# Two transformer layers on one core: GpSimd splits two early weight chunks and the router's weights first, and the other three early chunks after the layer norm

## The chip, the cores and the metric

The kernel runs on 1 core of a Trainium2 chip. The metric is the device time of one execution in microseconds (us), the median of several. The core has a matrix engine (TensorE, PE in the profile, with PEld for its weight loads), VectorE (DVE), ScalarE (ACT), GpSimd (POOL) and SyncE (SP), which here only issues DMA transfers. Each engine works through its own list of instructions in order, and waits on semaphores for the others.

## The reference, cut to what matters

Two layers, each an attention and a feed-forward part, each part added to its input and normalised (layer norm) behind it. Batch 2, sequence 1024, width 256, all in float32. The change lies at the end of the second layer's attention and the start of its feed-forward part, a mixture of experts:

```python
x = _layernorm(x + _L0_attn_ref(x, ...))
x = _layernorm(x + _L0_ffn_ref(x, W1, W2, W3))
x = _layernorm(x + _L1_attn_ref(x, Wq, bq, Wk, bk, Wv, bv, Wo, bo))
x = _layernorm(x + _L1_ffn_ref(x, w12, w3, router_w, expert_bias, sw1, sw2, sw3))

# _L1_ffn_ref
g = x @ sw1.T                                  # shared expert, 1024 wide
u = x @ sw2.T
shared_out = jax.nn.silu(g) * u @ sw3.T
scores = jax.nn.sigmoid(x @ router_w.T)        # router, 8 experts
_, top_idx = jax.lax.top_k(scores + expert_bias, 2)
...                                            # each token goes through its 2 experts, 128 wide
return shared_out + routed_out
```

## The kernel before

The two sequences of the batch are computed one after the other (`for b in range(B)`, B = 2); "batch 0" and "batch 1" below are these two passes. A pass holds 1024 rows of 256 in SBUF (`X`, 8 tiles of 128 rows) and goes through first attention, first feed-forward, second attention, second feed-forward. The order of the work on each engine is written out by hand, one block of code per engine.

**Products in three passes.** A float32 operand is split in a high part (rounded to the matrix engine's fp32r type) and a low part (the rest), and a product is the sum of high x high, high x low and low x high (`pass3`, lines 409 to 411). The high part is a cast, the low part a subtraction. So every weight has to be split before it is used: `Fw_h`, `Fw_l` are the parts of a feed-forward chunk, `E_h`, `E_l` of an expert, `Rw_h`, `Rw_l` of the router's weights, `XT_h`, `XT_l` of the transposed rows, `H_h`, `H_l` of the hidden values.

**The feed-forward chunks.** Both feed-forward parts go through chunks of 128 hidden columns: chunks 0 to 7 are the first part, 8 to 15 the second part's shared expert. A chunk (gate, up and down weights, 128x768) is loaded into `Fw_raw[c % 2]`, two buffers in turn, and split into one of five `Fw_h`, `Fw_l` slots. `load_chunk(b, c, ...)` on SP (line 693) waits until the chunk two before it has been split (`fw_lo`), since that one lay in the same buffer, and then issues two transfers (lines 695, 696). `EARLY` (line 87) names chunks 8 to 12: both their parts are made by GpSimd in `ffn_split` (line 2293, the cast on 2297, the subtraction in the helper `low` on 2255) at the end of the second attention. Chunks 13 to 15 are split later by ScalarE and VectorE.

**SP's list around the change** (lines 765 to 776): the loads for the second attention, the five `EARLY` chunks, then a wait for the residual sum (`z_done`), the router's constants `moe` and `tri_raw` (770, 771), the experts' weights `E_raw` in four transfers of two experts each (774), and chunks 13 to 15:

```python
for c in EARLY:
    load_chunk(b, c, d["fb"][c - CH_F0])
sp.wait_ge(z_done, LN_B * b + 3 * NT)
...
    sp.dma_start(E_raw[:, e], d["fe"][e].rearrange("e p n -> p e n")).then_inc(er_in[i], 16)
```

**The layer norm behind the second attention.** VectorE's `attn1_out` calls `add_norm`: for each of 8 tiles it adds the projected attention to `X` (`residual`, line 1662) and takes statistics (1667); after tile 5 it normalises tiles 0 to 3 (`layernorm(b, 2, 0)`, line 1683, four instructions, each raising `ln_done`), and after tile 7 it makes `XT_l` of the first 512 rows (`x_parts`, 1658) and normalises tiles 4 to 7. PE transposes normalised tiles in between (`transpose_x`, 816). While it has nothing else it issues products that are thrown away (`keep_clock`, 802).

**The shared expert.** Steps s = 16 to 31 (`S_SHARED` = 16) go over chunks 8 to 15: 16 to 19 are chunks 8 to 11 on the first 512 rows, 20 to 23 the same chunks on the other rows. PE's `ffn` (line 986): `gate_up(16)`, `gate_up(17)`, transposes of the other 512 rows, `gate_up(18)`, `router` (which waits in `wait_xt` for `XT_l` of the other rows, and for `rw_lo`), `down(16)`, `gate_up(19)`, and so on. ScalarE's `ffn` for each step: `silu` (1470); at step 17 also `x_parts` (1330, `XT_h` of the other 512 rows); `hidden_high` (1475); and for steps 16 to 19 `split_experts` (1505), which waits for transfer i of `E_raw` (`er_in`) and casts two experts. VectorE makes the products of gate and up (`Hf`, 1870), `XT_l` (1658) and `H_l` (1874). GpSimd makes `E_l`, and later issues the scatter of the tokens to their experts.

Of the kernel before, what the change touches and what calls it, by code (L numbers as in the profile page):

```python
# [35 lines left out]
NT = T // P  # L36
# [50 lines left out]
EARLY = range(CH_F0, CH_F0 + FW_RING)  # L87
# [8 lines left out]
def program(nc, d, ctx):  # L96
    def sem(name):
        return ctx.enter_context(nc.semaphore(name))

    def sb(name, shape, dt=F32, scope=ctx):  # L100
        return scope.enter_context(nc.sbuf_tensor(name, shape, dt))
# [111 lines left out]
    Rw_raw = sb("Rw_raw", [P, KC, P], F32, s)  # L213
    Rw_h = sb("Rw_h", [P, KC, P], F32R, s)
    Rw_l = sb("Rw_l", [P, KC, P], F32R, s)
# [53 lines left out]
    rw_in = sem("rw_in")  # L269
# [11 lines left out]
    ln_done = sem("ln_done")  # L281
# [54 lines left out]
    rw_hi = sem("rw_hi")  # L336
    rw_lo = sem("rw_lo")
# [272 lines left out]
    LN_B = 4 * NT  # L610
# [1642 lines left out]
    def _(pool):  # L2253
        def low(dst, full, high):
            return nc.gpsimd.tensor_tensor(dst, full, high.bitcast(F32), ALU.subtract)
# [13 lines left out]
        def attn0_group(b, g, last):  # L2269
            it = b * GROUPS0 + g  # L2270
            for n in range(STEPS0):
                w = (q_tile(n, last) + 1) * P
                e1, e2 = E1[n % 2][:, 0:w], E2[n % 2][:, 0:w]
                pool.wait_ge(mix_ready, STEPS0 * it + n + 1)
                pool.nop(nofuse=True)
                nc.gpsimd.tensor_scalar(e2, e2, mixc[:, n % 4:n % 4 + 1], 1.0, ALU.mult,  # L2276
                                        ALU.mult).then_inc(mix_scaled, 1)
                pool.wait_ge(mix_scaled, STEPS0 * it + n + 1)
                nc.gpsimd.tensor_tensor(e1, e1, e2, ALU.add).then_inc(p_ready, 1)  # L2279
                for t in v_tiles(n):  # L2280
                    pool.wait_ge(v_hi, NT * it + t + 1)
                    low(V_l[:, t, :].unsqueeze(1), O[:, t, bass.ds(g % 2 * 2 + 1, 1), :],
                        V_h[:, t, :].unsqueeze(1)).then_inc(v_lo, 1)
                if n in SPLIT_STEPS:
                    split_wa(it + 1, SPLIT_STEPS.index(n))
                if last and n == STEPS0 - 2:
                    scale_wo(it)
            if not last:
                scale_wo(it)
            pool.wait_ge(wo_hi, it + 1)  # L2290
            low(Wo_l[:], Wo_raw[:], Wo_h[:]).then_inc(wo_lo, 1)

        def ffn_split(b, c):
            if c in EARLY:
                pool.wait_ge(fw_in[c % 2], CHUNKS * 16 * b + (c + 2 - c % 2) * 16)
                pool.nop(nofuse=True)
                nc.gpsimd.tensor_copy(Fw_h[c % FW_RING][:], Fw_raw[c % 2][:]).then_inc(fw_early, 1)
                pool.wait_ge(fw_early, FW_RING * b + c - EARLY[0] + 1)
            else:
                pool.wait_ge(fw_hi, (CHUNKS - FW_RING) * b + (c if c < CH_F0 else c - FW_RING) + 1)  # L2300
            low(Fw_l[c % FW_RING][:], Fw_raw[c % 2][:], Fw_h[c % FW_RING][:]).then_inc(fw_lo, 1)
# [62 lines left out]
        for b in range(B):  # L2364
            attn0_group(b, 0, False)
            with pool.Fori(1, GROUPS0 - 1) as g:
                attn0_group(b, g, False)
            if b == 0:
                pool.wait_ge(const_in, CONSTS * 16)
            pool.wait_ge(y_added, 3 * NT * b + (GROUPS0 - 2) * NT)  # L2370
            add_bias(0)
            attn0_group(b, GROUPS0 - 1, True)
            attn0_out(b)
            ffn0(b)
            nc.gpsimd.memset(causal[:, 0:HALF - P], 0.0).then_inc(filled, 1)
            nc.gpsimd.tensor_copy(causal[:, HALF - P:], mask_r[:].bitcast(F32)).then_inc(filled, 1)
            pool.wait_ge(wv_hi, b + 1)
            low(Wv_l[:], Wv_raw[:], Wv_h[:]).then_inc(wv_lo, 1)
            split_wb(b)
            for n in range(NT):  # L2380
                pool.wait_ge(v1_done, NT * b + n + 1)
                values = Vs[:, n, :, 0:D1]
                nc.gpsimd.tensor_tensor(values, values, rows_bc[:, 2, :].rearrange("p (h e) -> p h e", h=HEADS1),
                                        ALU.add).then_inc(vb_done, 1)
            for p in range(PAIRS1):
                for j in CUT:
                    cut_future(PAIRS1 * b + p, p, j)
                    if j == CUT[0]:
                        if p == 0:
                            pool.wait_ge(xt_ps, LN_B // 2 * b + 12)  # L2390
                        add_tile_bias(p)
            for c in EARLY:
                ffn_split(b, c)
            pool.wait_ge(rw_in, 16 * b + 16)
            pool.wait_ge(rw_hi, b + 1)
            low(Rw_l[:], Rw_raw[:], Rw_h[:]).then_inc(rw_lo, 1)
            pool.wait_ge(moe_in, 32 * b + 32)
            pool.nop(nofuse=True)
            nc.gpsimd.tensor_copy(tri[:], tri_raw[:, 0:2 * P].rearrange("p (c n) -> p c n", c=2)).then_inc(tri_done, 1)
            nc.gpsimd.tensor_copy(X[:, :, HID], tri_raw[:, 2 * P:]).then_inc(tri_done, 1)  # L2400
            for e in range(EXPERTS):
                pool.wait_ge(er_hi, EXPERTS * b + e + 1)
                low(E_l[:, e], E_raw[:, e], E_h[:, e]).then_inc(er_lo, 1)
            pool.wait_ge(tri_done, 2 * b + 2)
            pool.wait_ge(xs_init, 16 * b + 16)
            pool.wait_ge(rt_dve, R_B * b + R_PLACE)
            pool.nop(nofuse=True)
            for t in range(NT):
                for c in range(TOP):
                    nc.gpsimd.indirect_dma_start(d["xs"], bass.IndirectOffsetOnAxis(place_i[:, c, t:t + 1], 0), X[:, t, :],  # L2410
                                                 None).then_inc(sc_out, 16)
            for k in range(TILES):
                if k in [ends[0] for ends in XG_LOADS]:
                    load = [ends[0] for ends in XG_LOADS].index(k)
                    pool.wait_ge(dest_done, 3 * len(XG_LOADS) * b + 3 * load + 3)
                    pool.nop(nofuse=True)
                pool.wait_ge(ry_copy, TILES * b + k + 1)
                pool.nop(nofuse=True)
                nc.gpsimd.indirect_dma_start(d["ys"], bass.IndirectOffsetOnAxis(dest_i[:, k:k + 1], 0), xg[:, k, 0:HID],
                                             None).then_inc(yr_out, 16)  # L2420
# [84 lines left out]
```

## Time and profile before

| | before |
|---|---|
| median of 3 runs | 1646.4 us |
| lowest and highest | 1642.59, 1650.22 us |
| the profiled execution: its own time | 1648.83 us |
| its span, first to last instruction | 1647.1 us |
| mean granted TensorE clock, share of full | 0.989 |
| busy: PE, DVE, ACT, POOL | 1542.6, 1101.2, 930.0, 695.7 us |

The profile is of one execution. Its page gives each engine's busy time and groups instructions by line; the timeline gives single instructions (or merged ones, with "x4") with their start, their time and, in brackets, how long the engine sat idle before and what released it; a view of windows gives busy time and the granted clock (PEclk, 1.00 is 2.4 GHz, 0.50 is 1.2 GHz) of stretches. The end of the second attention lies at 677 to 697 us for batch 0 and at 1489 to 1509 us for batch 1.

### The profile page before, as it was taken

To read this page: it belongs to the slowest core of one execution; us is meant where nothing else is said; L and a number is where in the kernel's file an instruction comes from. 1 tells how busy PE (TensorE), PEld (TensorE's weight loads), DVE (VectorE), ACT (ScalarE), POOL (GpSimd) and SP (SyncE) were. 2 spreads that over 40 slices of the span, in tenths; PEclk is the share of its full clock that TensorE was granted. 3 is DMA by queue.
4 is the path that set the end of the run, shared out by engine and by line. 5 is a ranking of instruction groups with operands and counts; after the bars stand their busy time and mean duration, and the time that the engine had idled before them with its cause. 6 is when DMAs were issued, how large, how long until landed. Compare 5 with 4: busy or idle time off the path is not lost.

```text
span 1647.1 us, 30890 instructions
## 1 busy us (share of the span) xinstructions
PE 1542.6 (94%) x10614; PEld 1331.6 (81%) x10614; DVE 1101.2 (67%) x2705; ACT 930.0 (56%) x2054; POOL 695.7 (42%) x756
## 2 busy tenths in 40 slices
PE   8999999999999999899898999999999999998985
PEld 7888889888888677588788898898988876667784
DVE  6767667677745888474577676676766377865555
ACT  5666565665544577552566655556554347774352
POOL 1635444654560222451535445444554512226531
PEclk9999999999999999999999999999999999999998
DMA  3110000020110422223210200000202123313133
GB/s 132 46 52 17 27 1 16 25 91 1 49 60 13 80 50 45 64 103 126 101 68 6 73 18 26 16 25 0 91 1 68 40 41 64 52 32 130 62 123 103
DMA packets 48195, 88.02 MB, mean 53 GB/s; under 512 B 9600, under 2 KB 30480, under 8 KB 46928
## 3 DMA queue, kind: packets, MB, share of 16 engines
q1 hardware_dynamic: 43552, 75.28, 15.9%
q0 software_dynamic: 3744, 10.26, 1.7%
q8 instruction: 76, 1.25, 0.3%
q10 hardware_dynamic: 768, 0.79, 0.2%
q14 instruction: 55, 0.45, 0.1%
HBM read 60.18 MB, written 19.76 MB: 49 GB/s over the span
## 4 chain that ended last, share of the span: by engine, by line
PE 64%; DVE 15%; ACT 10%; issue 7%; POOL 3%; ACTq 0%; DMA 0%; DVEq 0%; POOLq 0%; SPq 0%
PE ps L409 16%; PE ps L411 15%; PE ps L410 15%; PE ps L1214 4%; PE ps L1196 4%; PE ps L1161 3%; ACT E L1411 3%; DVE nmax L1810 3%; PE ps L924 2%; ACT PT L1572 2%; POOL E L2279 2%; DVE On L1728 2%; ACT PT_h L1393 1%; DVE PT_l L1785 1%; POOL E L2276 1%
## 5 line engine op out<-in xcount | busy, mean ns | idle before, releaser
L1411 ACT ACTIVATE E<-ps,nmax 128x128 f32<-128x128 f32 (+7 forms) x256 | 189.1, 741 | 208.5 <-DVE nmax L1810 208.1
L2276 POOL TENSOR_SCALAR E<-E,mixc 128x128 f32<-128x128 f32 (+7 forms) x128 | 97.1, 759 | 399.7 <-DVE mixc L1778 399.7
L1810 DVE TENSOR_REDUCE nmax<-ps 128x1 f32<-128x128 f32 (+7 forms) x256 | 183.3, 749 | 12.7 <-PE ps L901 12.6
L2279 POOL TENSOR_TENSOR E<-E 128x128 f32<-128x128 f32 (+7 forms) x128 | 182.4, 1425 | 10.7
L1572 ACT ACTIVATE PT<-ps 128x512 f32<-128x512 f32 x288 | 153.9, 602 | 57.3 <-PE ps L1196 56.5
L409 PE MATMUL ps<-V_h,PT_h 128*128 128x256 f32 x576 | 167.3, 290 | 1.7 <-DVE O L1790 1.7
L410 PE MATMUL ps<-V_l,PT_h 128*128 128x256 f32 x576 | 163.1, 283 | 0.0
L411 PE MATMUL ps<-V_h,PT_l 128*128 128x256 f32 x576 | 163.0, 283 | 0.0
L409 PE MATMUL ps<-K_h,Q_h 128*128 128x512 f32 (+3 forms) x384 | 147.4, 384 | 8.9 <-ACT E L1411 5.6
L2337 POOL TENSOR_SCALAR_AFFINE_SELECT PT<-PT 128x256 f32<-128x256 f32 (+1 forms) x160 | 57.0, 361 | 202.3 <-ACT PT L1572 201.0
L1785 DVE TENSOR_TENSOR PT_l<-ps,PT_h 128x128 fp32r<-128x128 f32 (+7 forms) x128 | 96.7, 756 | 60.7 <-ACT PT_h L1393 60.1
L411 PE MATMUL ps<-K_h,Q_l 128*128 128x512 f32 (+3 forms) x384 | 133.2, 347 | 0.0
L410 PE MATMUL ps<-K_l,Q_h 128*128 128x512 f32 (+3 forms) x384 | 132.7, 346 | 0.0
L2030 DVE CUSTOM_DVE_ANT_0 masked<-ps,causal 128x128 bf16<-128x128 f32 (+3 forms) x256 | 110.4, 487 | 33.3 <-PE ps L1161 33.1
L1161 PE MATMUL ps<-KS,QS 128*128 128x512 f32 (+3 forms) x384 | 114.2, 374 | 2.3 <-DVE nmax_part L2030 0.6
L409 PEld LDWEIGHTS ps<-V_h,PT_h 128*128 128x128 f32 x576 | 109.8, 191 | 3.5 <-issue 2.1
L1196 PE MATMUL ps<-QS,KS 128*128 128x512 f32 (+3 forms) x384 | 108.7, 363 | 3.0 <-ACT PT L1572 2.9
L410 PEld LDWEIGHTS ps<-V_l,PT_h 128*128 128x128 f32 x576 | 110.0, 191 | 0.5
L411 PEld LDWEIGHTS ps<-V_h,PT_l 128*128 128x128 f32 x576 | 109.8, 191 | 0.0
L409 PE MATMUL ps<-XT_h,Fw_h 128*128 128x512 f32 x256 | 103.7, 405 | 4.9 <-DVE XT_l L1658 2.2
L1870 DVE TENSOR_TENSOR Hf<-ps,silu_g 128x512 f32<-128x512 f32 x64 | 44.2, 691 | 91.5 <-PE ps L411 77.2
L411 PE MATMUL ps<-XT_h,Fw_l 128*128 128x512 f32 x256 | 102.2, 399 | 1.0 <-issue 1.0
(265 smaller groups left out, 4659.7 us busy)
## 6 DMA issues: line engine op xcount, KB each, us to landing
Wa_raw<-in_wa SPq DMA_DIRECT2D x8, 1024.0 KB, 6.0
Fw_raw<-in_fa SPq DMA_DIRECT2D x32, 256.0 KB, 2.6
E_raw<-in_fe SPq DMA_DIRECT2D x8, 768.0 KB, 7.3
xs<-in_xs SPq DMA_DIRECT2D x2, 2967.0 KB, 13.0
Wo_raw<-in_wo SPq DMA_DIRECT2D x8, 512.0 KB, 3.5
yg<-ys SPq DMA_DIRECT2D x8, 512.0 KB, 5.3
xg<-xs SPq DMA_DIRECT2D x6, 645.0 KB, 8.5
KS<-QK_h SPq DMA_DIRECT2D x56, 64.0 KB
```

The source lines that it names most:

```text
L409: nc.tensor.matmul(out, a_h, b_h, start=start, stop=False, **kw)
L410: nc.tensor.matmul(out, a_h, b_l, start=False, stop=False, **kw)
L411: return nc.tensor.matmul(out, a_l, b_h, start=False, stop=stop, **kw)
L1161: mm = nc.tensor.matmul(bank1(j % RING1)[:, at:at + z - a], QS[:, 2 * (p % Q_PAIRS) + n, tile(i)], KS[:, p % K_PAIRS, a:z], start=at == 0, ...
L1196: mm = nc.tensor.matmul(bank[:, at:at + z - a], KS[:, p % K_PAIRS, tile(kb)], QS[:, 2 * (p % Q_PAIRS) + n, a:z], start=k == 0, stop=True, ...
L1411: nc.scalar.activation(e[:, 0:w], ps[m][:, 0:w], ACT.Exp, bias=nmax[:, s % 4, m:m + 1], accum_out=lsum[:, s % 4, m:m + 1]).then_inc(exp_do ...
L1572: nc.scalar.activation(PT[:, at:at + HALF], bank1(RING1 + n % RING1), ACT.Exp, scale=SCALE1).then_inc(t_used, 1)
L1785: nc.vector.tensor_tensor(PT_l[n % 2][:, 0:w], ps[2][:, 0:w], PT_h[n % 2][:, 0:w].bitcast(F32), ALU.subtract).then_inc(pt_lo, 1)
L1810: nc.vector.tensor_reduce(nmax[:, s % 4, m:m + 1], ps[m][:, 0:(q_tile(s, last) + 1) * P], AX.X, ALU.max, negate=True).then_inc(nmax_ready[ ...
L2030: ins = nc.vector.tensor_tensor_reduce(out=masked[:, j % RING1, cols], in0=scores, in1=causal[:, HALF - (z - a):], scale=-1.0, scalar=3e38 ...
L2276: nc.gpsimd.tensor_scalar(e2, e2, mixc[:, n % 4:n % 4 + 1], 1.0, ALU.mult, ALU.mult).then_inc(mix_scaled, 1)
L2279: nc.gpsimd.tensor_tensor(e1, e1, e2, ALU.add).then_inc(p_ready, 1)
```

## The change

In GpSimd's list, the low part of the router's weights moves ahead of chunk 10 (`EARLY[2]`), and behind it stands a new wait: GpSimd does not go on to chunks 10, 11 and 12 before all eight tiles of the second attention's layer norm are normalised (`ln_done`). Nothing is added or removed, and no other engine's code is touched.

```diff
             for c in EARLY:
+                if c == EARLY[2]:
+                    pool.wait_ge(rw_in, 16 * b + 16)
+                    pool.wait_ge(rw_hi, b + 1)
+                    low(Rw_l[:], Rw_raw[:], Rw_h[:]).then_inc(rw_lo, 1)
+                    pool.wait_ge(ln_done, LN_B * b + 3 * NT)
                 ffn_split(b, c)
-            pool.wait_ge(rw_in, 16 * b + 16)
-            pool.wait_ge(rw_hi, b + 1)
-            low(Rw_l[:], Rw_raw[:], Rw_h[:]).then_inc(rw_lo, 1)
             pool.wait_ge(moe_in, 32 * b + 32)
```

GpSimd's list (POOL) from chunk 8 to the experts, before (the pairs of a cast and a subtraction are chunks 8 to 12):

```order
L2297 CAST Fw_h<-Fw_raw 128x768 [waits fw_in0]
L2255 TENSOR_TENSOR Fw_l<-Fw_raw,Fw_h 128x768 [waits fw_early]
L2297 CAST Fw_h<-Fw_raw 128x768 [waits fw_in1]
L2255 TENSOR_TENSOR Fw_l<-Fw_raw,Fw_h 128x768 [waits fw_early]
L2297 CAST Fw_h<-Fw_raw 128x768 [waits fw_in0]
L2255 TENSOR_TENSOR Fw_l<-Fw_raw,Fw_h 128x768 [waits fw_early]
...
L2255 TENSOR_TENSOR Rw_l<-Rw_raw,Rw_h 128x256 [waits rw_hi,rw_in]
L2399 CAST tri<-tri_raw 128x256 [waits moe_in]
```

and now:

```order
L2255 TENSOR_TENSOR Fw_l<-Fw_raw,Fw_h 128x768 [waits fw_early]
L2255 TENSOR_TENSOR Rw_l<-Rw_raw,Rw_h 128x256 [waits rw_hi,rw_in]
L2297 CAST Fw_h<-Fw_raw 128x768 [waits ln_done,fw_in0]
L2255 TENSOR_TENSOR Fw_l<-Fw_raw,Fw_h 128x768 [waits fw_early]
L2297 CAST Fw_h<-Fw_raw 128x768 [waits fw_in1]
L2255 TENSOR_TENSOR Fw_l<-Fw_raw,Fw_h 128x768 [waits fw_early]
L2297 CAST Fw_h<-Fw_raw 128x768 [waits fw_in0]
L2255 TENSOR_TENSOR Fw_l<-Fw_raw,Fw_h 128x768 [waits fw_early]
L2401 CAST tri<-tri_raw 128x256 [waits moe_in]
```

`Rw_l` stands three chunks earlier, and chunk 10's cast has a second semaphore, `ln_done`. SP's list is the same in both kernels; from the load of chunk 11 on it reads:

```order
L695 DMA Fw_raw<-in_fa 128x512 [waits fw_lo]
L696 DMA Fw_raw<-in_fb 128x256
L695 DMA Fw_raw<-in_fa 128x512 [waits fw_lo]
L696 DMA Fw_raw<-in_fb 128x256
L770 DMA moe<-in_moe 128x120 [waits z_done]
L771 DMA tri_raw<-in_tri 128x264
L774 DMA E_raw<-in_fe 128x2x768 x4
L695 DMA Fw_raw<-in_fa 128x512 [waits fw_lo]
```

The first two rows load chunk 11, the next two chunk 12. The `fw_lo` of the third row asks for chunk 10's split. ScalarE's list is also the same in both; from step 16's silu to step 18's:

```order
L1470 ACTIVATE silu_g<-ps 128x512 [waits gate_mm]
L1475 CAST H_h<-Hf 128x512 [waits gu_used,down_mm]
L1505 CAST E_h<-E_raw 128x768 [waits y1_mm,er_in0]
L1505 CAST E_h<-E_raw 128x768
L1470 ACTIVATE silu_g<-ps 128x512 [waits gu_used,gate_mm]
L1330 CAST XT_h<-ps 128x2x256 [waits xt_ps] x2
L1475 CAST H_h<-Hf 128x512 [waits gu_used,down_mm]
L1505 CAST E_h<-E_raw 128x768 [waits er_in1]
L1505 CAST E_h<-E_raw 128x768
L1470 ACTIVATE silu_g<-ps 128x512 [waits gu_used,gate_mm]
```

Nothing moved here; the third row waits for the first transfer of `E_raw`.

## Rows read from the trace of the kernel before

**Rows 1.** The page: busy time and share of each engine

```profile
PE 1542.6 (94%) x10614; PEld 1331.6 (81%) x10614; DVE 1101.2 (67%) x2705; ACT 930.0 (56%) x2054; POOL 695.7 (42%) x756
```

**Rows 2.** Timeline, DVE, batch 0: start us, us, engine line op

```profile
689.30 3.41 DVE L1683 TENSOR_SCALAR X<-X,mv,rstd 128x256 f32<-128x256 f32 x4
```

**Rows 3.** Timeline, POOL, batch 0, chunk 12's subtraction

```profile
689.70 1.80 POOL L2255 TENSOR_TENSOR Fw_l<-Fw_raw,Fw_h 128x768 fp32r<-128x768 f32 x1
```

**Rows 4.** Timeline, DVE, batch 1, the same stage

```profile
1503.38 1.38 DVE L1683 TENSOR_SCALAR X<-X,mv,rstd 128x256 f32<-128x256 f32 x4
...
1508.18 1.38 DVE L1683 TENSOR_SCALAR X<-X,mv,rstd 128x256 f32<-128x256 f32 x4
...
1515.30 1.28 DVE L1658 TENSOR_TENSOR XT_l<-ps,XT_h 128x512 fp32r<-128x512 f32 x2
```

**Rows 5.** Timeline, POOL, batch 1

```profile
1500.11 0.82 POOL L2297 CAST Fw_h<-Fw_raw 128x768 fp32r<-128x768 f32 x1
1501.01 1.85 POOL L2255 TENSOR_TENSOR Fw_l<-Fw_raw,Fw_h 128x768 fp32r<-128x768 f32 x1
1502.82 0.74 POOL L2255 TENSOR_TENSOR Rw_l<-Rw_raw,Rw_h 128x256 fp32r<-128x256 f32 x1
```

**Rows 6.** Timeline, PE, batch 0: transposes, step 16, the router

```profile
691.70 0.74 PE L816 MATMUL ps<-ident,X 128*128 128x128 f32 x4 [2.08 <-DVE X L1683]
...
696.63 0.39 PE L409 MATMUL ps<-XT_h,Fw_h 128*128 128x512 f32 x1
...
705.94 0.40 PE L409 MATMUL ps<-XT_h,Rw_h 128*128 128x512 f32 x1
```

**Rows 7.** Timeline, PE, batch 1: step 16, the router

```profile
1508.12 0.51 PE L409 MATMUL ps<-XT_h,Fw_h 128*128 128x512 f32 x1 [0.58 <-DVE XT_l L1658]
...
1517.51 0.40 PE L409 MATMUL ps<-XT_h,Rw_h 128*128 128x512 f32 x1
```

**Rows 8.** Timeline, SP's queue, batch 1

```profile
1497.12 0.33 SPq L695 DMA_DIRECT2D Fw_raw<-in_fa  x1
1497.50 0.43 SPq L696 DMA_DIRECT2D Fw_raw<-in_fb  x1
1505.78 0.33 SPq L770 DMA_DIRECT2D moe<-in_moe  x1
...
1506.62 2.06 SPq L774 DMA_DIRECT2D E_raw<-in_fe  x4
```

**Rows 9.** E_raw's first transfer, issue to landing: batch 1, then batch 0

```profile
DMA to landing us min/median/max: 5.5/5.5/5.5
...
DMA to landing us min/median/max: 4.4/4.4/4.4
```

**Rows 10.** Timeline, ACT, batch 1, steps 16 and 17

```profile
1512.08 0.62 ACT L1475 CAST H_h<-Hf 128x512 fp32r<-128x512 f32 x1 [1.66 <-DVE Hf L1870]
1512.61 1.56 ACT L1505 CAST E_h<-E_raw 128x768 fp32r<-128x768 f32 x2
1514.08 0.59 ACT L1470 ACTIVATE silu_g<-ps 128x512 f32<-128x512 f32 x1
```

**Rows 11.** Windows: us, busy per engine, PEclk, DMA share, GB/s

```profile
689.60:691.70 2.10, 0.03 (x1) 0.00 (x0) 2.10 (x3) 0.00 (x0) 2.02 (x3) 1.00 0.00 0
691.70:696.60 4.90, 4.58 (x17) 3.68 (x18) 4.76 (x16) 2.75 (x4) 0.53 (x1) 0.65 0.26 50
...
818.80:821.60 2.80, 2.75 (x7) 2.17 (x8) 1.29 (x2) 1.07 (x2) 0.00 (x0) 0.50 0.43 96
```

**Rows 12.** Timeline, PE, batch 1's first products, after an idle stretch

```profile
818.85 0.79 PE L409 MATMUL ps<-XT_h,Wa_h 128*128 128x512 f32 x1 [2.62 <-DVE XT_l L1658]
...
821.58 0.52 PE L409 MATMUL ps<-XT_h,Wa_h 128*128 128x512 f32 x1
```

**Rows 13.** Timeline, POOL and DVE, batch 1, around the scatter of tokens

```profile
1527.17 3.65 POOL L2255 TENSOR_TENSOR E_l<-E_raw,E_h 128x768 fp32r<-128x768 f32 x2 [1.89 <-ACT E_h L1505]
...
1541.19 1.08 POOL L2410 DMA_INDIRECT xs<-X,place_i  x1 [10.37 <-DVE past L2156]
```

## The prediction, made before the changed kernel ran

> **What bounds the kernel now.** I read the page first: PE is busy 94% of the span and no other engine above 67% [rows 1], so time is gained or lost where PE waits. The change touches one place per batch, so I went to the timelines of that place, engine by engine, in both batches, which run the same code and differ in when GpSimd finishes its splits.
>
> In batch 0 VectorE's first four normalising instructions take 3.41 us together [rows 2]; in batch 1 the same four take 1.38 us [rows 4]. In batch 0 GpSimd's subtraction for chunk 12 runs from 689.70 to 691.50 us [rows 3], inside them; in batch 1 it ended at 1502.86 [rows 5], before they began at 1503.38. So the two engines get in each other's way, and in batch 0 alone. PE waits for these instructions: 2.08 us before its transposes [rows 6]. And in the stretch behind this idle time its granted clock averages 0.65 [rows 11], which slows the products it issues until step 16.
>
> From there PE has no gap until the router's products: step 16 to router takes 705.94 - 696.63 = 9.31 us in batch 0 [rows 6] and 1517.51 - 1508.12 = 9.39 in batch 1 [rows 7]. Whatever delays the router's products delays the end.
>
> **Part one: the collision goes.** With chunks 10 to 12 behind the layer norm and the router's low part done long before it, GpSimd is silent while VectorE normalises. The direct gain in batch 0 is 3.41 - 1.38 = 2.03 us. The whole gain, with the clock, is read from the two batches' distance between the first normalising instruction and step 16: 696.63 - 689.30 = 7.33 us in batch 0 [rows 2, 6], 1508.12 - 1503.38 = 4.74 in batch 1 [rows 4, 7]. So step 16 comes **2.59 us** earlier in batch 0. In batch 1 the gain is **0**. There the router's subtraction (1502.82 to 1503.56, rows 5) overlaps the first normalising instruction by 0.18 us, and the four take no more than the next four at 1508.18 [rows 4]. The Trainium skill (SBUF — State Buffer, Who interferes with whom) calls the port that VectorE and GpSimd share an exclusive lock, held by whoever starts first for the whole instruction. By that rule batch 1 would also gain, 0.18 us; batch 0 agrees with it, batch 1's row shows no such wait, and I keep 0.
>
> Moving the router's subtraction itself costs nothing: 0.74 us [rows 5] on a GpSimd that then waits, and PE wants it some 20 us later.
>
> **Part two: what is queued behind chunk 10's split.** Chunks 10 and 11 themselves are not late for PE. Their loads land before the norm as now, a chunk takes 2.75 us on GpSimd (1500.11 to 1502.86, rows 5), so in batch 1 chunk 10 is ready at 1512.3, while step 18, which wants it, is the last of the three steps between 1508.12 and 1517.51 [rows 7] and begins near 1514.
>
> But SP's list is in order, and chunk 12's load waits for chunk 10's split. Behind that load stand the router's constants and all the experts' weights `E_raw`. Today the load is issued at 1497.12, and `E_raw` at 1506.62, held by the residual sum alone [rows 8]. ScalarE casts the first two experts at 1512.61, directly behind step 16's `H_h` [rows 10], when the first transfer has just landed, 1506.62 + 5.5 = 1512.1 [rows 8, 9]. So there is 0.5 us of slack, and the change puts about 7 us on this transfer. ScalarE is in order too: behind the two casts stand step 17's silu and `XT_h` of the other 512 rows, without which neither `XT_l` nor the router's products can start.
>
> The chain in batch 1, from the last normalising instruction's end, 1508.18 + 1.38 = 1509.56 [rows 4]:
> - GpSimd splits chunk 10: 2.75, to 1512.3 [rows 5].
> - SP issues chunk 12's two transfers: 1497.12 to 1497.93, 0.81 [rows 8]. Then constants until `E_raw`: 1506.62 - 1505.78 = 0.84 [rows 8]. `E_raw` is issued at 1513.96.
> - It lands 5.5 later [rows 9], at 1519.46.
> - ScalarE: from the casts' start to step 17's silu 1514.08 - 1512.61 = 1.47 [rows 10]. From that silu to the end of `XT_l`, 1515.30 + 1.28 - 1514.08 = 2.50 [rows 4, 10].
>
> The sum is 13.87 us: `XT_l` at 1523.4, where the router's products start at 1517.51 now. **Batch 1 loses 5.9 us.** In batch 0 the norm now ends at 689.30 + (1509.56 - 1503.38) = 695.48; plus 13.87 is 709.35, against 705.94 now [rows 6]. **Batch 0 loses 3.4 us, the gain of part one already in it.** (Without that gain it would be 6.0.)
>
> The uncertain link is the landing. Chunk 12's 384 KB now go shortly ahead of `E_raw`, and batch 0's first transfer landed in 4.4 [rows 9]. I take batch 1's 5.5, the row with the usual issue of the constants, with 4.4 and 6.5 (another us of queueing, from the distance of the two rows) as bounds: -1.1 to +1.0 us per batch. By the fit in the Trainium skill (DMA: Bandwidth & Descriptors, Anatomy of one DMA, there given for GpSimd's path), 2.0 us plus the bytes over 436 GB/s, an `E_raw` transfer of 786 KB would land in 3.8 us, an estimate; the loss would be 1.7 us less per batch. Both rows are above that, and the sum goes by the rows.
>
> **Part three: the clock.** PE stands idle some 6 us ahead of the router's products. The nearest row is the idle time of 2.62 us ahead of batch 1's first products [rows 12]: behind it the granted clock was 0.50, that is 1.2 GHz, for the stretch of 2.8 us [rows 11], and the first six products of 512 columns began over 821.58 - 818.85 = 2.73 us. At full clock, step 16 to router is 36 such products and eight transposes in 9.31 us [rows 6], so at most 0.26 us each, 1.55 for six. That is **1.2 us lost per batch**. The bounds are 0 (the clock holds) and twice this, 2.4.
>
> **Off the path.** The moved splits and then `E_l` overlap VectorE's `H_l` subtractions and may stretch them, but `down(16)`, which wants the first, stands behind the router's products. The work behind these products moves with them: the last `E_l` pair ends at 1530.82, the scatter starts at 1541.19, 10.37 us of GpSimd idle ended by VectorE's routing [rows 13]. Both follow PE's step 19 and keep their distance. Batch 1 ends with this part, and batch 0's delay is passed on through engines that follow PE, so I give nothing back.
>
> **Sum.** 3.4 + 5.9 + 2 x 1.2 = **11.7 us**. Against the profiled execution's own 1648.8 us (span 1647.1) that is 1660.5. The median of the runs lies 2.4 us lower, at 1646.4, so I forecast **1658.1 us**, 0.7% slower.
>
> **Rivals.**
> - *Only the collision goes* (not slower): the experts' weights are not late, or ScalarE is not held by them. Then the kernel gains batch 0's 2.6 us: 1643.8. It decides if `E_raw`'s first transfer has landed before ScalarE is through with step 16's `H_h`, at about 1512.6 in batch 1; for it speaks that the collision is real. Against it: SP's order and the 0.5 us of slack. 7%.
> - *The wait is free when it is met*: `ln_done` might be at its count already, so that only the router's subtraction moves. That keeps the collision with chunks 10 to 12 and gives 1646.4. The count is 24 per batch below 32 in all, three norms of eight tiles, so it is met by this norm's last tile. 1%.
> - *Part of the delay is absorbed*, by work later on that waits today for something other than PE (the scatter's transfers): a loss of 3 to 7 us, about 1651. 8%.
> - *More than the chain*: `E_raw` shares the DMA engines with chunks 12 and 13, its later transfers hold steps 17 and 18 too, or `E_l` starts so late that it passes its 10.37 us of slack [rows 13] and holds the scatter. 5 us on top give 1663. 6%.
>
> The forecast has 78%.
>
> **How the numbers follow.** A measurement of this kernel tells about 0.5% from no change, 8.2 us; the line is at 1654.6. The forecast's own bounds are 11.7 - 2.2 - 2.4 = 7.1 and 11.7 + 2.0 + 2.4 = 16.1 us, so 1653.5 to 1662.5; the three runs spread by 4 us to either side of their median, so medians may be off by 1 to 2. The range is 1652 to 1665. Of the forecast's 78% some 8 lie below the line, the last rival's 6% above it: slower 76%. Of the first rival's 7%, 2 are for a collision that costs far more than its rows show: faster 2%. Within 0.5%: 8 + 5 + 1 + 8 = 22%.
>
> **What the changed profile would show.** Right: both batches' normalising instructions at 1.38 us for four; GpSimd idle from the router's subtraction to the norm's end (695.5 in batch 0); chunk 12's load issued 2.8 us after the norm's end and `E_raw` 1.7 us behind it; ScalarE idle some 6 to 7 us, released by a DMA, before the first experts' cast; PE idle about 6 us before the router's products, and a clock of 0.50 behind it. The forecast is wrong if the casts of the experts start directly behind step 16's `H_h`, if PE meets the router without a gap, or if the scatter's distance to PE shrinks by what was lost.

## The result, and the profile after

| | before | after |
|---|---|---|
| median of 4 runs each, the same chip | 1647.83 us | 1662.48 us |
| lowest, highest | 1642.59, 1650.22 | 1655.6, 1664.85 |
| ratio to before, 95% interval | | 1.0087 [1.0054, 1.012] |
| profiled execution, its span | 1648.83, 1647.1 | 1655.6, 1653.9 |

The change costs 14.65 us by the medians. (Of all executions on these pages one, of casts_later below, took 1867.29 us at a mean granted clock of 0.748, and its median and ratio are those of its other five.) The busy times of the engines hardly move (PE 1542.6 before [rows 1]); the time lost is time in which PE waits.

The page of the changed kernel, busy time and share of each engine:

```profile
PE 1538.8 (93%) x10614; PEld 1326.1 (80%) x10614; DVE 1098.9 (66%) x2705; ACT 929.1 (56%) x2054; POOL 696.4 (42%) x756
```

**The gain is there.** The timeline of VectorE in the changed kernel (start us, us, engine, line, op), the first four normalising instructions of batch 0 and of batch 1: 1.38 us in both, where batch 0 took 3.41 before [rows 2].

```profile
688.98 1.38 DVE L1683 TENSOR_SCALAR X<-X,mv,rstd 128x256 f32<-128x256 f32 x4
...
1503.93 1.38 DVE L1683 TENSOR_SCALAR X<-X,mv,rstd 128x256 f32<-128x256 f32 x4
```

Read one by one, the 3.41 us of before hold two delays, where an instruction of this kind takes 0.41 us by itself:

```profile
689.69 1.96 DVE L1683 TENSOR_SCALAR X<-X,mv,rstd 128x256 f32<-128x256 f32 x1
...
691.57 0.82 DVE L1683 TENSOR_SCALAR X<-X,mv,rstd 128x256 f32<-128x256 f32 x1
```

The first ends with chunk 12's subtraction (691.50, rows 3), the second lies beside the router's, which ran from 691.46 to 692.24. So both subtractions that the change moves away were in the collision, not chunk 12's alone.

**And so is the loss, link by link.** GpSimd's timeline in batch 0 (in brackets the idle time ahead and what ended it). The router's low part ends at 682.65, and chunk 10's split begins when the last row is normalised, after 12.68 us of idle time:

```profile
681.91 0.74 POOL L2255 TENSOR_TENSOR Rw_l<-Rw_raw,Rw_h 128x256 fp32r<-128x256 f32 x1
695.33 0.83 POOL L2297 CAST Fw_h<-Fw_raw 128x768 fp32r<-128x768 f32 x1 [12.68 <-DVE X L1683]
696.24 1.84 POOL L2255 TENSOR_TENSOR Fw_l<-Fw_raw,Fw_h 128x768 fp32r<-128x768 f32 x1
```

SP's queue in batch 0. Chunk 12's load follows the split's end (696.24 + 1.84 = 698.08) at once, the constants and the experts' weights stand behind it; in batch 1 `E_raw` goes out at 1514.85, where it went at 1506.62 [rows 8]:

```profile
698.11 0.33 SPq L695 DMA_DIRECT2D Fw_raw<-in_fa  x1
...
698.95 0.43 SPq L770 DMA_DIRECT2D moe<-in_moe  x1
...
699.90 2.48 SPq L774 DMA_DIRECT2D E_raw<-in_fe  x4
```

ScalarE, batch 0 and then batch 1. After step 16's `H_h` it waits for the first of these transfers, 7.58 and 9.16 us; in batch 1 of before the cast followed `H_h` with no wait [rows 10]. The silu of step 17 and the other rows' `XT_h` stand behind it:

```profile
697.67 0.62 ACT L1475 CAST H_h<-Hf 128x512 fp32r<-128x512 f32 x1 [1.66 <-DVE Hf L1870]
705.87 1.56 ACT L1505 CAST E_h<-E_raw 128x768 fp32r<-128x768 f32 x2 [7.58 <-DMA E_raw<-in_fe]
707.35 0.59 ACT L1470 ACTIVATE silu_g<-ps 128x512 f32<-128x512 f32 x1
...
1522.41 1.56 ACT L1505 CAST E_h<-E_raw 128x768 fp32r<-128x768 f32 x2 [9.16 <-DMA E_raw<-in_fe]
```

PE: step 16 of batch 0, then the router's first products of both batches, with 6.72 and 8.30 us of idle time ahead of them where there was none [rows 6, 7]. The next products take 0.63 us, where the first of before took 0.40:

```profile
693.72 0.50 PE L409 MATMUL ps<-XT_h,Fw_h 128*128 128x512 f32 x1 [0.58 <-DVE XT_l L1658]
...
710.00 0.76 PE L409 MATMUL ps<-XT_h,Rw_h 128*128 128x512 f32 x1 [6.72 <-DVE XT_l L1658]
710.56 0.63 PE L410 MATMUL ps<-XT_l,Rw_h 128*128 128x512 f32 x1
...
1526.54 0.77 PE L409 MATMUL ps<-XT_h,Rw_h 128*128 128x512 f32 x1 [8.30 <-DVE XT_l L1658]
```

The windows of the changed kernel (stretch, length, busy time of PE, PEld, DVE, ACT, POOL; then PEclk, DMA share, GB/s). The granted clock is 0.50, that is 1.2 GHz, from before the router's products until some time after 714:

```profile
708.00:710.00 2.00, 0.00 (x1) 0.03 (x1) 2.00 (x4) 2.00 (x4) 2.00 (x2) 0.51 1.03 406
710.00:712.00 2.00, 2.00 (x5) 1.61 (x6) 1.52 (x2) 1.37 (x3) 2.00 (x2) 0.50 1.04 389
712.00:714.00 2.00, 2.00 (x7) 1.52 (x6) 1.26 (x2) 1.81 (x3) 2.00 (x2) 0.50 0.51 178
714.00:716.00 2.00, 2.00 (x12) 1.76 (x11) 2.00 (x3) 0.27 (x1) 2.00 (x2) 0.78 0.00 0
```

**How much, measured in place.** The table gives distances between the starts of instructions in the profiled executions: from the first normalising instruction to step 16 on PE, on to the router's first product, on to the ranking of the picks (PE, `both` by `tri`); and their sum, added up before rounding. "xg" is the distance from SP's first load of the tokens, once they are sorted by expert, to PE's transposes of the first expert's; no edit here touches its two ends. It can be compared on one chip only: kernels that lose nothing have 20.0 (before) and 18.9 (rw_only) on two chips, and 15.5 (wait_at_12) on a third.

| kernel | batch 0: norm, step 16, router, rank | sum | xg | batch 1 | sum |
|---|---|---|---|---|---|
| before | 7.3 + 9.3 + 18.1 | 34.8 | 20.0 | 4.7 + 9.4 + 18.1 | 32.2 |
| after | 4.7 + 16.3 + 20.4 | 41.4 | 18.6 | 4.7 + 17.9 + 20.0 | 42.6 |
| half_dose | 4.7 + 14.7 + 20.7 | 40.2 | 15.4 | 4.7 + 13.0 + 18.2 | 35.9 |
| load12_behind | 4.7 + 9.4 + 24.2 | 38.3 | 16.5 | 4.7 + 9.4 + 24.0 | 38.1 |
| casts_later | 4.8 + 9.4 + 21.0 | 35.1 | 13.4 | 4.7 + 9.4 + 21.0 | 35.1 |
| split12_behind | 4.7 + 9.4 + 21.0 | 35.2 | 17.7 | 4.8 + 9.4 + 21.0 | 35.2 |
| wait_at_12 | 4.8 + 9.4 + 18.1 | 32.3 | 15.5 | 4.7 + 9.4 + 18.1 | 32.2 |
| rw_only | 7.1 + 9.3 + 18.1 | 34.6 | 18.9 | 6.8 + 9.4 + 18.1 | 34.3 |

Batch 0 loses 6.6 us and batch 1 loses 10.4, in all 17.0; 1.4 come back in batch 0's xg. That leaves 15.7 beside the 14.65 of the medians. The two profiled executions themselves differ by only 6.8 us, and this is no contradiction: from batch 0's last stage to batch 1's norm, where nothing was changed, before's execution took 684.1 us and after's 677.4. In before's the clock fell in stretches where after's held it; at 876 us, for instance, the windows of before and of after read

```profile
876.00:880.00 4.00, 4.00 (x23) 4.00 (x22) 1.89 (x3) 2.12 (x6) 1.35 (x2) 0.57 0.00 0
```

```profile
876.00:880.00 4.00, 1.88 (x18) 1.77 (x17) 2.86 (x6) 2.47 (x8) 3.73 (x3) 1.00 0.00 0
```

A second profile of the changed kernel, on another chip (after_again below), took 683.0 there and 1661.0 in all, 13.9 more than before. One profiled execution against another says little about 0.5% of this kernel. The distances in place repeat within some 0.2 us but for one: from step 16 to the router batch 1 took 16.6 us there for 17.9, since its first transfer of `E_raw` landed 6.2 us after its issue and not 7.5.

### The profile page after: what moved, and what is told of

Same layout as the page of the kernel before. It is cut to its first block, busy times and chain, and to the rows that moved or that the text cites. A ratio compares the mean times of both kernels' runs of the same rounds, so it can differ in the third digit from the quotient of the medians.

```text
span 1653.9 us, 30890 instructions
## 1 busy us (share of the span) xinstructions
PE 1538.8 (93%) x10614; PEld 1326.1 (80%) x10614; DVE 1098.9 (66%) x2705; ACT 929.1 (56%) x2054; POOL 696.4 (42%) x756
## 4 chain that ended last, share of the span: by engine, by line
PE 62%; DVE 15%; ACT 10%; issue 7%; POOL 3%; DMA 1%; ACTq 0%; SPq 0%; DVEq 0%; another core or an unknown queue 0%; POOLq 0%
PE ps L409 16%; PE ps L411 15%; PE ps L410 14%; PE ps L1214 4%; PE ps L1196 4%; PE ps L1161 3%; ACT E L1411 3%; DVE nmax L1810 3%; PE ps L924 2%; ACT PT L1572 2%; POOL E L2279 2%; DVE On L1728 2%; ACT PT_h L1393 1%; DVE PT_l L1785 1%; POOL E L2276 1%
## 5 line engine op out<-in xcount | busy, mean ns | idle before, releaser
L924 PE MATMUL ps<-ident,E 128*128 128x128 f32 x576 | 85.1, 275 | 18.7 <-POOL E L2279 18.5
```

What stands on the lines that cost most here:

```text
L924: mm = nc.tensor.transpose(ps[2][:, tile(kb)], E1[n % 2][:, tile(kb)], ident[:])
```

## The experiments

The theory: the collision of GpSimd with VectorE's norm is gone as drawn, worth 2 to 3 us; the loss is SP's list in its order, by which the wait ahead of chunk 10 delays chunk 12's load and so `E_raw`, ScalarE's casts, the second half of `XT` and the router. Rivals: GpSimd's own lateness is the price; the idle clock is most of it; the moved router split matters. Three chips were used, with their own level of before: 1626.45 us (load12_behind, wait_at_12, casts_later, half_dose), 1645.2 (after_again, keep_clock, rw_only), 1627.21 (the other four). Ratios are to before on the same chip, with 95% intervals; they are not the plain quotients of the medians.

**load12_behind.** The changed kernel, but SP loads chunk 12 after `E_raw`; the wait stays.

```diff
-            for c in EARLY:
+            for c in EARLY[:-1]:
                 load_chunk(b, c, d["fb"][c - CH_F0])
...
-            for c in range(EARLY[-1] + 1, CHUNKS):
+            for c in range(EARLY[-1], CHUNKS):
```

> The change, with chunk 12's load moved on SP behind the four transfers of the experts' weights; nothing is left out. Theory (SP's list holds E_raw behind chunk 10's split, ScalarE waits for it, PE waits for ScalarE): E_raw is issued at the residual sum again, the first experts' cast stands directly behind step 16's H_h, PE has no gap before the router's products. Both batches lose nothing and batch 0 keeps its 2.6 us: about 2.6 us below before, ratio 0.998. Rival (the late splits on GpSimd, or their hold on VectorE, cost the time): about as slow as the change, ratio 1.009.

Measured: 1638.11 us, 1.0074 [1.0061, 1.0087]. The link is as the theory has it: step 16 to router is back at 9.4 us, and ScalarE's timeline shows the casts directly behind `H_h`:

```profile
697.65 0.63 ACT L1475 CAST H_h<-Hf 128x512 fp32r<-128x512 f32 x1 [1.66 <-DVE Hf L1870]
698.18 1.57 ACT L1505 CAST E_h<-E_raw 128x768 fp32r<-128x768 f32 x2
```

But the time was forecast below before's, and it is 11.7 us above. The table says where: router to rank takes 24 us instead of 18. GpSimd now gets chunk 12 late, and then has all eight subtractions of the experts in one piece (its timeline, batch 0):

```profile
704.89 0.82 POOL L2297 CAST Fw_h<-Fw_raw 128x768 fp32r<-128x768 f32 x1 [3.82 <-DMA Fw_raw<-in_fb]
...
708.40 14.88 POOL L2255 TENSOR_TENSOR E_l<-E_raw,E_h 128x768 fp32r<-128x768 f32 x8
```

They lie beside VectorE's routing, of whose instructions of some 0.2 us many then take 1.2 to 1.8 us:

```profile
714.32 1.84 DVE L2117 TENSOR_SCALAR ta<-ta 128x64 f32<-128x64 f32 x1
...
716.78 1.22 DVE L2119 TENSOR_TENSOR sel<-sc,rbias 128x64 f32<-128x64 f32 x1
718.03 0.22 DVE L2120 TENSOR_REDUCE tm<-sel 128x8 f32<-128x64 f32 x1
718.29 1.52 DVE L2122 TENSOR_TENSOR ta<-sel,tm 128x64 f32<-128x64 f32 x1
719.84 1.76 DVE L2123 TENSOR_TENSOR ta<-ta,first 128x64 f32<-128x64 f32 x1
```

PE then waits for the picks:

```profile
727.29 0.21 PE L1033 MATMUL ps<-both,tri 128*128 128x64 bf16 x1 [6.21 <-DVE both L2134]
```

So there are two chains. In the changed kernel the first hides the second: PE is so late at the router that GpSimd is nearly through when the routing begins. With the first cut, the second takes its place and asks much of the same price. Against wait_at_12 on the same chip the distances up to the rank grow by 11.9 us and xg by 1.0; 13.3 were measured. The part of the theory that made the order of SP's list the whole cause fell.

**wait_at_12.** The changed kernel with the wait ahead of chunk 12 alone.

```diff
                     low(Rw_l[:], Rw_raw[:], Rw_h[:]).then_inc(rw_lo, 1)
+                if c == EARLY[-1]:
                     pool.wait_ge(ln_done, LN_B * b + 3 * NT)
```

> The change, but with the wait for the layer norm ahead of chunk 12 alone; chunks 10 and 11 are split before the norm. Theory: chunk 12's load is issued when chunk 10 is split, before the norm, so E_raw is on time, and the subtraction that collided in batch 0 is still kept off the norm: batch 0 gains 2.6 us, batch 1 nothing, ratio 0.998. Rival (any split behind the norm costs): a third to a whole of the change's loss, ratio 1.003 to 1.009.

Measured: 1624.85 us, 0.9992 [0.9983, 1.0001], 11 runs. Norm, router and rank all at their shortest in both batches. GpSimd's wait of 7.27 us is left. Of the loads it holds only chunk 14's, issued at 697.97 behind `E_raw`, and nothing that PE waits for in this stage:

```profile
686.08 1.85 POOL L2255 TENSOR_TENSOR Fw_l<-Fw_raw,Fw_h 128x768 fp32r<-128x768 f32 x1
695.20 0.83 POOL L2297 CAST Fw_h<-Fw_raw 128x768 fp32r<-128x768 f32 x1 [7.27 <-DVE X L1683]
```

All of the loss therefore comes from holding chunks 10 and 11, whose splits free the buffers for the loads of chunks 12 and 13; that chunk 12's split is held too costs nothing here. A wait ahead of chunk 11 was not run; by SP's list only chunk 10's split stands ahead of `E_raw`. A second set of runs, **wait_at_12_again**, on another chip:

> The wait ahead of chunk 12 alone once more, beside the other three: 0.998 to 1.000, as its first measurement of 0.9992 and the profile's 2.6 us in batch 0 say.

Measured: 1625.6 us against 1627.21, 0.9994 [0.9985, 1.0003]. The collision is gone in the profile (1.38 us for four), but the medians give 1.6 us in both sets, and neither interval excludes none.

**casts_later.** The other way to free the router: ScalarE casts the experts at steps 18 to 21 instead of 16 to 19.

```diff
-                if S_SHARED <= s < S_SHARED + ER_LOADS:
-                    split_experts(b, s - S_SHARED)
+                if S_SHARED + 2 <= s < S_SHARED + 2 + ER_LOADS:
+                    split_experts(b, s - S_SHARED - 2)
```

> The change, with ScalarE's casts of the experts' weights at steps 18 to 21 instead of 16 to 19; E_raw is as late as in the change. Theory (ScalarE's list is the link): step 17's silu and XT_h are no longer behind the wait for E_raw, PE's gap before the router's products goes, and nearly the whole loss with it: within 3 us of before, ratio 0.997 to 1.002. Rival (the late transfer costs through the DMA engines or GpSimd's E_l): the loss stays, ratio 1.006 or more.

Measured: 1633.48 us, 1.0057 [1.004, 1.0074]. The forecast, within 3 us of before, missed: it is 7.0 us above. The router's gap is gone here too (9.4 us), which shows that ScalarE's order is a link of the chain. The second chain takes over again: the late `E_l` meet two later steps of the routing,

```profile
721.09 1.59 DVE L2129 TENSOR_TENSOR ta<-sel,tm 128x64 f32<-128x64 f32 x1
722.71 1.73 DVE L2130 TENSOR_TENSOR ta<-ta,first 128x64 f32<-128x64 f32 x1
```

router to rank is 21.0 us, and rank to the scatter takes 8.2 us for 5.6. Against wait_at_12 on the same chip these distances give 2.9 us per batch ahead of the rank and 2.6 behind, 10.9 in all, of which xg returns 2.1; that is 8.8, and 8.6 were measured.

**half_dose.** The kernel before, with GpSimd's code untouched; SP alone waits for the norm ahead of chunk 12's load. This delays `E_raw` by about 3 us less than the change does, and delays chunk 12's split with it.

```diff
             for c in EARLY:
+                if c == EARLY[-1]:
+                    sp.wait_ge(ln_done, LN_B * b + 3 * NT)
                 load_chunk(b, c, d["fb"][c - CH_F0])
```

> The kernel before, GpSimd's list untouched, but SP waits for the layer norm's end ahead of chunk 12's load. E_raw is then issued 1.7 us behind the norm's end, 2.75 us earlier than in the change and 4 to 5 us later than before. Theory: the same chain with a smaller delay. Batch 0 +1.8, batch 1 +4.6, and about 2 us of lower clock in each: 10.4 us, ratio 1.006. Rival (it is GpSimd's splits): no loss, ratio 0.999 (chunk 12's split also leaves the norm).

Measured: 1638.98 us, 1.008 [1.0067, 1.0093], 12.5 us for the 10.4 forecast. The gaps ahead of the router are smaller than the change's, in PE's timeline:

```profile
711.94 0.77 PE L409 MATMUL ps<-XT_h,Rw_h 128*128 128x512 f32 x1 [5.13 <-DVE XT_l L1660]
...
1514.44 0.47 PE L409 MATMUL ps<-XT_h,Rw_h 128*128 128x512 f32 x1 [3.43 <-DVE XT_l L1660]
```

So a late `E_raw` makes the gap without GpSimd's wait. The gaps differ as the landings do: the first transfer of `E_raw` landed 7.3 us after its issue in batch 0 and 5.6 in batch 1. Against wait_at_12 the distances up to the rank grow by 7.9 and 3.6 us, 11.5 in all. The medians differ by 14.1, so 2.6 us are not found in place (in the profiled execution the norm itself began at 692.5 us, 3.7 later than wait_at_12's, behind a stretch at a clock of 0.50 from 682 to 686, where wait_at_12's was 1.00; that lies ahead of everything that this edit reaches). It also gives the clock's price by itself: the windows of this kernel behind the two gaps,

```profile
711.90:714.00 2.10, 2.06 (x5) 1.71 (x6) 1.61 (x2) 1.42 (x3) 2.10 (x2) 0.50 0.82 294
...
1514.40:1516.40 2.00, 1.96 (x9) 1.63 (x10) 1.51 (x2) 1.42 (x3) 2.00 (x2) 1.00 1.04 392
```

behind the 5.13 us gap the clock was 0.50 and router to rank took 20.7 us; behind the 3.43 us gap it was 1.00 and the same distance was 18.2.

**after_again.** The changed kernel on the chip of the next two.

> The change once more, beside the next three on the same chip: ratio near the first measurement's 1.009. By its chain, read from its profile, batch 0 loses about 6.6 us and batch 1 about 10.4, so 17 us or 1.010.

Measured: 1661.69 us, 1.0107 [1.0089, 1.0126]. The result repeats.

**keep_clock.** The changed kernel, with 26 products ahead of the router whose result is thrown away (work added that the kernel doesn't need), so that PE isn't idle.

```diff
             pe.wait_ge(rw_lo, b + 1)
+            keep_clock(ring[0], 26)
             wait_xt(b, 3, 1)
```

> The change, with 26 products of 512 columns, thrown away, on PE between step 18 and the router's products, in the gap where PE stands idle. Theory (the gap costs its length, and about 2 us per batch more through a granted clock of 0.50 behind it): the gap stays as long, the clock stays at 1.00, and about 4 us of the 17 come back: ratio 1.007. Rival (the clock costs nothing that is not hidden): same as the change.

Measured: 1655.4 us, 1.0071 [1.0056, 1.0086]; 6.3 us less than after_again by the medians. In batch 0 the added products fill the gap and the clock holds (PE's timeline, then the window):

```profile
703.29 6.09 PE L802 MATMUL ps<-ident_r 128*128 128x512 f32 x26
709.83 0.50 PE L409 MATMUL ps<-XT_h,Rw_h 128*128 128x512 f32 x1 [0.45 <-DVE XT_l L1659]
```

```profile
710.00:712.00 2.00, 2.00 (x9) 1.63 (x10) 1.57 (x2) 1.30 (x3) 2.00 (x2) 1.00 1.03 378
```

Router to rank is 18.2 us there, against 20.5 in after_again: the clock's price is **2.3 us** in batch 0. In batch 1 the 26 products end 1.8 us too early and the clock falls all the same, behind the router's first products: they take 0.50 and 0.39 us, the later ones 0.63.

```profile
1524.04 0.50 PE L409 MATMUL ps<-XT_h,Rw_h 128*128 128x512 f32 x1 [1.81 <-DVE XT_l L1659]
1524.37 0.39 PE L410 MATMUL ps<-XT_l,Rw_h 128*128 128x512 f32 x1
...
1524.94 0.63 PE L409 MATMUL ps<-XT_h,Rw_h 128*128 128x512 f32 x1
```

The distance from router to rank stays at 19.8 there. Up to the rank keep_clock is 2.7 us shorter than after_again in batch 0 and 0.7 longer in batch 1, so in place it explains 2.0 of the 6.3 us. Of the two profiled executions the rest lies in the unchanged middle of the program (676.7 against 683.0 us), where after_again's clock fell at three places (884, 1365 and 1498 us) and keep_clock's at none. It is not these two executions alone: the mean granted clock is 0.985 to 0.989 in after_again's six and 0.990 to 0.994 in keep_clock's. But rw_only, which has no added products, took 677.0 us in the middle and had no fall there either. What decides where the clock falls in the middle was not settled, so a part of the change's loss may lie there. What is settled: without the clock's drop in batch 0 the kernel is still 0.7% slower, and behind the two gaps the clock is the smaller part (2.3 and 1.9 us of the 17.0 in place).

**rw_only.** The router's low part ahead of chunk 10, with no wait.

```diff
                     low(Rw_l[:], Rw_raw[:], Rw_h[:]).then_inc(rw_lo, 1)
-                    pool.wait_ge(ln_done, LN_B * b + 3 * NT)
                 ffn_split(b, c)
```

> Only one part of the change: the router's subtraction ahead of chunk 10, without the wait. Theory: E_raw is on time, so none of the loss. The later chunks move by 0.75 us: in batch 0 the four normalising instructions (from 689.3 us, one each 0.33 us) then begin before chunk 12's subtraction (690.4), so they should be clear of it and the gain of 2.6 us comes without any wait: ratio 0.998. Rival (the subtraction meets them all the same, or batch 1's norm is met by chunk 12 instead): ratio 1.000 to 1.001.

Measured: 1643.44 us, 1.0000 [0.998, 1.0019]. The move is free and gains nothing, as the prediction's second rival has it. It even brings the collision into batch 1: with the router's split out of the way chunk 12's cast and subtraction run at the time of the norm there as well. In batch 0, where only chunk 12's subtraction now meets the four instructions, they take 2.98 us for 3.41. GpSimd's and VectorE's timelines of batch 1:

```profile
1497.94 1.80 POOL L2255 TENSOR_TENSOR Fw_l<-Fw_raw,Fw_h 128x768 fp32r<-128x768 f32 x1
```

```profile
1496.44 3.45 DVE L1683 TENSOR_SCALAR X<-X,mv,rstd 128x256 f32<-128x256 f32 x4
```

**split12_behind.** load12_behind with the second chain shortened: GpSimd does six of the experts first, and chunk 12's split and the copies of `tri` only then.

```diff
-            for c in EARLY:
+            for c in EARLY[:-1]:
...
             for e in range(EXPERTS):
+                if e == EXPERTS - 2:
+                    ffn_split(b, EARLY[-1])
+                    pool.wait_ge(moe_in, 32 * b + 32)
...
                 pool.wait_ge(er_hi, EXPERTS * b + e + 1)
```

> The kernel with chunk 12's load behind the experts' weights, and now also its split (and the routing constants' copy) later on GpSimd: after six of the eight E_l. Theory (there the loss only moved: GpSimd's eight E_l ran from 708.4 us in one piece and met VectorE's routing, so router to rank products took 24.2 us instead of 18.1): E_l starts some 7 us earlier, leaves only two to meet the routing as before the change, and router to rank takes 18 to 19 us. The total is that of the wait at chunk 12, ratio 0.998 to 1.000. Rival (the 24.2 us come from late chunk transfers, not from E_l): it stays above 22 us, ratio 1.006.

Measured: 1634.68 us, 1.0047 [1.0033, 1.006], where 0.998 to 1.000 was forecast. Router to rank fell from 24.2 to 21.0, about half of what was expected. GpSimd is now busy with one thing or another throughout the routing:

```profile
702.39 11.79 POOL L2255 TENSOR_TENSOR E_l<-E_raw,E_h 128x768 fp32r<-128x768 f32 x6
714.14 1.29 POOL L2297 CAST Fw_h<-Fw_raw 128x768 fp32r<-128x768 f32 x1
715.51 1.85 POOL L2255 TENSOR_TENSOR Fw_l<-Fw_raw,Fw_h 128x768 fp32r<-128x768 f32 x1
...
717.79 3.66 POOL L2255 TENSOR_TENSOR E_l<-E_raw,E_h 128x768 fp32r<-128x768 f32 x2
```

Each of its subtractions still meets one of VectorE's instructions (1.38, 1.34, 1.75 and 1.51 us), and PE waits 3.03 us. Against wait_at_12_again the distances up to the rank give 5.8 us and xg another 2.2 (17.7 for 15.5); 9.1 were measured. By these rows it is the amount of GpSimd's work left when the routing begins that counts for the second chain, more than its order.

**joined_alone.** Before already has a small collision of this kind: the last two `E_l` meet the routing (1.30 and 1.52 us on VectorE at 716.25 and 717.84; after has the same at 722.58 and 724.17). Here before, with the last two transfers' casts both at step 18, so that GpSimd has no gap ahead of them.

```diff
-                if S_SHARED <= s < S_SHARED + ER_LOADS:
-                    split_experts(b, s - S_SHARED)
+                for i in {S_SHARED: (0,), S_SHARED + 1: (1,), S_SHARED + 2: (2, 3)}.get(s, ()) if first else ():
+                    split_experts(b, i)
```

> The kernel before, with ScalarE's casts of the last two experts pulled up to step 18, where it idles 2.4 us before step 19's silu. Theory: the last two E_l run about 1.9 us earlier and meet one of the two routing instructions that they meet now (1.30 and 1.52 us instead of 0.22 each), so about 1.3 us less per batch, ratio 0.998. Rival (the stall only moves to another routing instruction, or PE has slack there): 1.000.

Measured: 1627.32 us, 1.0002 [0.9993, 1.0012], as the rival has it. The eight run in one piece from 704.20 to 720.03, and the held instructions are now two others (`H_l` 1.24 us, the routing's first 1.84). Router to rank is 18.0 against 18.1: PE has that slack anyway.

**casts_joined.** wait_at_12 and joined_alone together.

```diff
+                if c == EARLY[-1]:
                     pool.wait_ge(ln_done, LN_B * b + 3 * NT)
...
-                if S_SHARED <= s < S_SHARED + ER_LOADS:
-                    split_experts(b, s - S_SHARED)
+                for i in {S_SHARED: (0,), S_SHARED + 1: (1,), S_SHARED + 2: (2, 3)}.get(s, ()) if first else ():
+                    split_experts(b, i)
```

> Both: the wait ahead of chunk 12 alone, and the last experts' casts at step 18. The gains add if they are what they are taken for: batch 0's 2.6 us and 1.3 us per batch, 5.2 us in all, ratio 0.997. Rival (either gain is not on the path): 0.998 to 1.000.

Measured: 1623.91 us, 0.998 [0.9971, 0.9989], 11 runs: 3.3 us faster than before, and the only version here whose interval lies below 1. Its distances up to the rank are those of wait_at_12 (18.0 for 18.1 from router to rank). Its lead over wait_at_12_again, 1.7 us on the same chip, has no row that explains it, and their intervals overlap, so that a gain from the casts was not shown.

## Why the prediction was right, and where it was off

It forecast 1658.1 us, 0.7% slower, from a sum of 11.7; 1662.48 was measured, a loss of 14.65, inside the range. In place the loss was 17.0 us, above the sum's upper bound of 16.1, so the time agrees better than the sum does.

- **The collision goes, 2.59 us in batch 0, nothing in batch 1.** Right: the norm to step 16 is 4.7 us in both batches, for 7.3 in batch 0 before. rw_only shows the reverse, a collision brought into batch 1 (6.8 us). The reading was short of one thing: batch 0's four instructions met the router's subtraction too (0.82 us for 0.41), not only chunk 12's.
- **SP's order.** Right in each link: in batch 0 chunk 12's load goes out 2.95 us behind the norm's end (2.75 were forecast) and `E_raw` 1.79 behind that (1.65), ScalarE stands, the router is late. half_dose makes the same gap from SP alone; load12_behind and casts_later each cut one link and each brings 9.4 us back.
- **The landing, 5.5 us.** Here the sum was mis-sized. The first transfer landed 6.0 us after its issue in batch 0 and 7.5 in batch 1, and ScalarE's cast began at 5.97 and 7.56. The bounds were 4.4 and 6.5, and batch 1 lies outside. The prediction took its two rows from transfers with no other load close ahead (chunk 12's was issued 9.6 and 9.5 us earlier), and here chunk 12's goes out 1.8 us ahead. load12_behind is the changed kernel with that load behind `E_raw`, and its first transfers landed after 4.5 and 5.4 us. The other kernels agree: with the load 1.8 us ahead the first transfer took 5.6 to 7.5 us (after, after_again, half_dose, casts_later, keep_clock), and in the other eight profiles 4.3 to 5.6. Why it takes 5.6 in one place and 7.5 in another is open. The median of all `E_raw` transfers went from 7.3 to 8.9 us. This is 0.5 and 2.1 of the 5.3 us by which the measured 17.0 exceeds the sum of 11.7.
- **The clock, 1.2 us per batch.** Mis-sized too: 2.3 (batch 0) and 1.9 (batch 1), within the bound of 2.4. The row that it came from [rows 12] was read only up to its sixth product; here eleven products of 512 columns go at the low clock. Another 1.8 us.
- **The rest of the 5.3, some 1.0 us,** is 0.5 per batch in small pieces: 0.2 and 0.14 us in the two just named, and 2.65 for 2.50 from step 17's silu to the router's first product.
- **Nothing given back.** Nearly: batch 0's xg gave 1.4 us in this pair of executions, and 0.5 on the other chip (18.5 in after_again, 18.9 in rw_only). So the rival "part of the delay is absorbed" (a loss of 3 to 7 us) did not come true. The scatter came 5.6 us behind the rank, as before, and GpSimd's idle time ahead of it is 10.42 us in batch 0, where it was 10.37 in batch 1 before [rows 13].
- **Rival "more than the chain".** It put GpSimd's late `E_l` on top. In the changed kernel it is not there: router to rank is 20.4 us, and the clock explains all above 18.1: with the clock kept (keep_clock, batch 0) it is 18.2. But the rival named a real chain, one that shows when the first is cut (24.2 us in load12_behind). The prediction weighed it by its 10.37 us of slack to the scatter; what it runs into first is VectorE's routing.
- **Rival "only the collision goes".** wait_at_12 is that case, and gives 0.9992 where 2.6 us would be 0.9984. Its interval holds both that and no gain. In place the 2.6 us are there; how much of them reaches the end stays open.

## What to carry to other kernels

A wait put into one engine's list holds everything behind it, and where that engine frees buffers, it holds the loader's list too, with every later load in it, whatever it is for. Follow the buffer first, then the queue behind the load. Put such a wait as late in the list as the collision allows: one chunk of work held instead of three took the 0.9% of loss away (0.9992, interval up to 1.0001). And before a link of a chain is cut, look for what is late right behind it: here a second chain stood behind the first, and neither cut that freed the router and left GpSimd late (load12_behind, casts_later) brought the kernel back to where it was. A landing time read where nothing else is being loaded is too short for a place where another load goes out just ahead.

## What the runs showed of the hardware

- A VectorE instruction with its operands in SBUF that meets a GpSimd subtraction mostly ends about when that subtraction ends: 0.22 us become 1.2 to 1.84. A GpSimd cast of 0.90 us held one in the same way (0.92 us at 1497.09 in rw_only). Reductions and the reciprocal beside it kept their 0.22 and 0.55 us (load12_behind: 718.03, 721.63 and 716.19), and so did `Hf`, which reads PSUM (0.69 us at 711.79 in split12_behind).
- The clock fell to 0.50 at idle stretches of PE of 5.13, 6.72, 6.99 and 8.30 us, and router to rank then took 1.7 to 2.6 us more. The length alone doesn't tell: it held at one of 3.43 us (half_dose, batch 1) and fell at shorter ones, 2.62 [rows 12] and 1.81 (keep_clock, batch 1). Filling the stretch with products up to the last 0.45 us kept it at 1.00.
- The same program's clock falls for some us at different places in different executions (before at 818, 876, 1357 and 1491 us, the changed kernel's first profile at none of these, its second at 884, 1365 and 1498). The same middle stretch took 676.7 to 677.4 us in the three profiles without such a fall (keep_clock, rw_only, after) and 683.0 and 684.1 in the two with (after_again, before).
- The first `E_raw` transfer of 786 KB landed 4.3 to 5.6 us after its issue with no other load close ahead, and 5.6 to 7.5 us when one of 393 KB had gone out 1.8 us earlier.
